# Cross-attention on one core: probabilities times V in bursts of four key tiles instead of two, six slots for exponentials instead of four

## The reference

```python
q = (x @ Wq + bq).reshape(B, N, NUM_HEADS, HEAD_DIM)      # N = 512, 16 heads of 32
k = (y @ Wk + bk).reshape(B, M, NUM_HEADS, HEAD_DIM)      # M = 8192, y has 384 features
v = (y @ Wv + bv).reshape(B, M, NUM_HEADS, HEAD_DIM)
scores = jnp.einsum('bnhd,bmhd->bhnm', q, k) * scale
attn = jax.nn.softmax(scores, axis=-1)
out = jnp.einsum('bhnm,bmhd->bnhd', attn, v).reshape(B, N, IMAGE_DIM)
```

## Time and profile before

| | |
|---|---|
| three runs, median | 3089.53 us (3088.96 to 3091.1) |
| profiled execution, span from first to last instruction | 3087.4 us |
| what lies around the span, against the median | 2.1 us |
| TensorE busy, matmul records | 2999.9 us, 97% of the span |
| VectorE busy | 2224.9 us, 72% |
| GpSimd busy | 1964.1 us, 64% |
| ScalarE busy | 1696.0 us, 55% |

### The profile page before, as it was taken

How to read it: one execution, slowest core, us unless ns; L and a number is a source line. 1 busy time by engine, 2 the same in 40 slices (tenths; PEclk the granted TensorE clock), 3 DMA queues, 4 the chain that set the end, 5 groups by cost and what they waited for, 6 DMA issues and landing times.

```text
span 3087.4 us, 41451 instructions
## 1 busy us (share of the span) xinstructions
PE 2999.9 (97%) x15408; PEld 1839.2 (60%) x15408; DVE 2224.9 (72%) x3416; ACT 1696.0 (55%) x2968; POOL 1964.1 (64%) x678
## 2 busy tenths in 40 slices
PE   7999999999999999999999999999999977899999
PEld 4666666666666666666666666666634333344477
DVE  7777777777777777777777777777746799986653
ACT  1566666666666666666666666666641555330021
POOL 1689898989889898988989898989860000000000
PEclk9999999999999999999999999999999988999999
DMA  5422322233223233232223222232231122224100
GB/s 165 121 53 73 75 75 63 63 77 73 73 53 81 69 97 94 63 85 65 73 52 88 62 73 63 72 84 58 48 136 47 42 69 96 65 72 165 68 14 17
DMA packets 100683, 230.13 MB, mean 75 GB/s; under 512 B 22850, under 2 KB 27970, under 8 KB 99234
## 3 DMA queue, kind: packets, MB, share of 16 engines
q1 hardware_dynamic: 99908, 226.71, 27.1%
q10 hardware_dynamic: 576, 0.79, 0.1%
HBM read 114.46 MB, written 8.06 MB: 40 GB/s over the span
## 4 chain that ended last, share of the span: by engine, by line
PE 91%; DVE 6%; ACT 2%; issue 1%; DMA 0%; SPq 0%; ACTq 0%; DVEq 0%
PE ps L1814 16%; PE ps L1853 15%; PE ps L1840 15%; PE ps L1767 9%; PE ps L1791 9%; PE ps L1798 9%; PE ps L2057 4%; PE ps L2021 4%; PE ps L1865 4%; PE ps L2037 3%; DVE bx L1303 1%; PE ps L1826 1%; PE ps L1822 1%; DVE bx L1249 1%; PE ps L2049 1%
## 5 line engine op out<-in xcount | busy, mean ns | idle before, releaser
L1040 DVE TENSOR_REDUCE pm<-ps 128x1 f32<-128x512 f32 x2048 | 1407.4, 691 | 486.9 <-PE ps L1814 412.3
L1522 ACT ACTIVATE pf<-ps 128x512 f32<-128x512 f32 x2048 | 1216.1, 600 | 722.3 <-PE ps L1840 632.8
L891 POOL TENSOR_TENSOR psum<-psum,pf 128x2048 f32<-128x2048 f32 x254 | 1165.7, 4589 | 107.3 <-ACT pf L1522 94.8
L1814 PE MATMUL ps<-ks,qs 96*128 96x512 f32 x2048 | 844.4, 412 | 4.7 <-DVE pm L1040 2.3
L1840 PE MATMUL ps<-qs,ks 98*128 98x512 f32 x2048 | 812.8, 398 | 2.5 <-ACT pf L1522 2.3
L891 POOL TENSOR_TENSOR psum<-pf 128x2048 f32<-128x2048 f32 x127 | 582.0, 4582 | 42.5 <-ACT pf L1522 41.5
L1814 PEld LDWEIGHTS ps<-ks,qs 96*128 96x128 f32 x2048 | 386.6, 189 | 222.8 <-issue 159.1
L1853 PE MATMUL ps<-pf,V 128*32 128x512 f32 x4096 | 494.2, 600 | 0.0
L1840 PEld LDWEIGHTS ps<-qs,ks 98*128 98x128 f32 x2048 | 390.6, 191 | 49.5 <-ACT pf L1522 11.3
L902 POOL PARTITION_ALL_REDUCE qstat<-qstat x2 | 0.7, 366 | 608.3 <-DVE qstat L1339 608.3
L1791 PE MATMUL ps<-cTh,Wkg 128*128 128x512 f32 x732 | 293.0, 400 | 2.6
(11 more groups left out here) (221 smaller groups left out, 3181.3 us busy)
## 6 DMA issues: line engine op xcount, KB each, us to landing
ks<-KH SPq DMA_DIRECT2D x512, 128.0 KB, 2.4
ks<-KL SPq DMA_DIRECT2D x256, 128.0 KB, 2.4
cT<-in_ctxT SPq DMA_DIRECT2D x32, 768.0 KB, 4.7
Wkg<-wk_rows SPq DMA_DIRECT2D x61, 384.0 KB, 3.0
BC<-bc_rows SPq DMA_DIRECT2D x32, 512.0 KB, 4.8
ring<-in_ffn_w SPq DMA_DIRECT2D x16, 1024.0 KB, 7.8
wA<-in_W_fcT SPq DMA_DIRECT2D x4, 1024.0 KB, 11.3
wB<-in_W_projT SPq DMA_DIRECT2D x4, 1024.0 KB, 7.0
```

The costliest lines, as they stand in the source:

```text
L891: pool.tensor_tensor(acc, before, pf[:, tile % P_SLOTS, :], ALU.add).then_inc(s_sum, 1)
L1040: dve.tensor_reduce(pm[:, n // BLK, n % BLK:n % BLK + 1], src, AX.X, ALU.max).then_inc(s_wfree, 1)
L1522: act.activation(pf[:, tile % P_SLOTS, j * NTOK:(j + 1) * NTOK], ps[:, S_BANK + u % S_BANKS, :], ACT.Exp, scale=SCALE).then_inc(s_exp, 1)
L1814: last = pe.matmul(dst, qs[0:3 * HD, h, t * P:(t + 1) * P], ks[0:3 * HD, keys_of(of, j), i * 512:(i + 1) * 512], start=True, stop=True)
```

## The change

`BURST` goes from 2 to 4 and `P_SLOTS` from 4 to 6. Bursts stand at steps 0 and 16 only, each with four key tiles and the denominators of the run of four tiles before; at steps 8 and 24, where a burst of two tiles with denominators stood, there is none. ScalarE copies the denominators out at step 17 instead of 9 (the condition uses BURST), and D, their transposition, moves from step 16, behind the burst, to step 22. For the last group both keep their places. The last line makes room in on-chip memory for two more slots of `pf`.

```diff
--- before.py
+++ after.py
@@ -71,6 +71,7 @@
 SB_AHEAD = 2
 M_STEP = UPG - 6
 T_LAG = UPG + 15
+D_LAG = 7
@@ -89,8 +90,8 @@
 LOW_AT = {2: (0, 0), 3: (1, 2)}
-P_SLOTS = 4
-BURST = 2
+P_SLOTS = 6
+BURST = 4
 BURSTS = NGT * MT // BURST
 NSUM = 4
 RUNS = NGT * MT // NSUM
@@ -98,7 +99,7 @@
 ADDS = NSUM - 1
 STEPS = (NGT - 1) * UPG + T_LAG + 2
 ATTENDED = UNITS - UPG + T_LAG - UPG + 2
-TURNED = UNITS + BURST * HG + 2
+TURNED = UNITS + 10
@@ -136,8 +137,14 @@
-    if i >= T_LAG and (i - T_LAG) % UPG < 2 and (i - T_LAG) // UPG < NGT:
-        items.append((("T", "D")[(i - T_LAG) % UPG], (i - T_LAG) // UPG))
+    g, r = divmod(i - T_LAG, UPG)
+    if 0 <= g < NGT and r == 0:
+        items.append(("T", g))
+    g, r = divmod(i - T_LAG - D_LAG, UPG)
+    if 0 <= g < NGT - 1 and r == 0:
+        items.append(("D", g))
+    if i == STEPS - 1:
+        items.append(("D", NGT - 1))
     return items
@@ -1565,8 +1572,10 @@
                 if i % UPG == 1 and 1 <= i // UPG <= NGT:
                     take_out(i // UPG - 1)
-                if i % UPG == BURST * HG + 1 and 1 <= i // UPG <= NGT:
+                if i % UPG == BURST * HG + 1 and 1 <= i // UPG < NGT:
                     take_sums(i // UPG - 1)
+                if i == UNITS + 9:
+                    take_sums(NGT - 1)
@@ -2191,7 +2200,7 @@
-    nc = _bacc.Bacc("TRN2", target_bir_lowering=False, num_devices=1)
+    nc = _bacc.Bacc("TRN2", target_bir_lowering=False, num_devices=1, dynamic_dma_scratch_size=256)
```

## The result

| | before | after |
|---|---|---|
| median | 3090.1 us (3089.0 to 3091.1, 4 runs) | 3202.1 us (3201.2 to 3207.9, 4 runs) |
| ratio after / before | | 1.0367, 95% interval 1.0353 to 1.0382 |
| span of the profiled execution | 3087.4 us | 3200.2 us |
| one group, from M to M, mean of 58 | 34.60 us | 36.43 us |
| last M of the loop to the start of the last denominators | 36.7 us | 36.7 us |

The prediction was 3202 us. All of the 113 us between the spans lie in the attention loop: 61 groups that are 1.83 us longer make 112 us, and what comes behind the loop has kept its length.

The account below looks back on a forecast made before the run. TensorE's starts were taken to bound the attention loop. The terms -41 - 10 + 62 + 85 + 16 = +112 us moved the median from 3089.5 to 3202 us, with a range of 3165 to 3240.

Parts of the forecast that it names:

- fewer bursts: Attention loop: bursts fall from 256 to 128, each saving 0.32 us of going in and coming out; 41 us saved.
- V copy at step 0: Denominators follow the four tiles, so the V copy lies beside them and 28 TensorE waits go; 10 us saved.
- hand-over at step 8: Side bank from K to V without a covering burst: V starts 1.0 us late in 62 groups; 62 us lost.
- hand-over at step 24: V starts 1.4 us late behind `KL`, half taken earlier by the A of step 25; 61 groups, 85 us lost.
- D at step 22: Away from a burst, D waits 0.22 us for a reduction and costs 0.26 us more, 62 times; 16 us lost.
- tail: Last two groups and tail: counted at 0 (-3 to +5), having no side work.
- What bounds the kernel: Attention loop: time is the sum of TensorE's starts; nothing else matters until a TensorE item must wait.
- Hidden hand-overs: Rival: the hand-overs at steps 8 and 24 stay hidden and the time falls to 3055 us; 5%.
- only one of them visible: Rival: only one hand-over shows, 3117 us (step 24 hidden) or 3140 (step 8 hidden); 4%.
- GpSimd as the bound: Rival: GpSimd's adds come 1 us late for the burst in each group, 62 us on top, 3264 us; 3%.
- The clock: Rival: TensorE's idling in the attention loop lowers the granted clock to 0.94, about 130 us on top, 3330 us; 3%.

Follow-up runs that it names:

- experiment 8: Experiment 6 with the sign change `nm` of the new maximum done by ScalarE in step 14 instead of VectorE; 3102.3 us.
- experiment 9: Experiment 8 with bursts of two key tiles instead of four; 3127.5 us.
- experiment 1: The changed kernel with bursts of two key tiles again, six slots and D at step 22 kept; 3109.1 us.
- experiment 2: The changed kernel with D moved from step 22 to behind the burst at step 0, ten steps later; 3193.5 us.
- experiment 3: The changed kernel with VectorE computing only the first 128 of 512 columns of `KL`, the rest zero; 3154.3 us.
- experiment 4: The changed kernel with all side work eight steps earlier, K taken out at steps 0 and 16, under the bursts; 3116.2 us.
- experiment 6: Experiment 5 with M moved from step 24 to step 16, ahead of a burst, and A 8 steps further ahead; 3393.4 us.
- experiment 12: Experiment 11 with T moved from step 15 to step 17, behind the burst, D again at step 0; 3088.9 us, ratio 0.9996 to before.
- experiment 5: The changed kernel with experiments 4 and 2 together, VectorE emptying D after `KL`; 3112.5 us.
- experiment 7: Experiment 6 with bursts of two key tiles instead of four; 3335.8 us.
- experiment 11: Experiment 8 with the first three casts of a context half spread over steps and `save_out` behind the keys; 3095.6 us.
- experiment 10: Experiment 6 with the sign change `nm` as a two-input VectorE instruction, -2 x mn + mn; single run, 3395.4 us.

## Why the prediction was right, point by point

| Term | predicted, us | measured |
|---|---|---|
| fewer bursts | -41 | 5.10 us from scores to scores, as worked out; -42 by the ordinary groups of experiments 8 and 9 (0.69 x 61) |
| V copy at step 0 | -10 | before, 28 first K pieces end 0.36 us late (10 us), in the changed kernel none; the 28 waits return in experiment 1 |
| hand-over at step 8 | +62 | 1.01 us late in the timeline, 62 x 1.01 = 63 |
| hand-over at step 24 | +85 | 1.40 us late, 61 x 1.40 = 85, half of it by the A |
| D at step 22 | +16 | 0.20 us in the timeline = 12; 16 in the loop by experiment 2 |
| tail | 0 | 0.4 us |
| sum | +112 | +112.0 (medians), 95% interval 109 to 118 |

**What bounds the kernel.** Right. TensorE's starts set the time, and no other engine became the bound: experiment 3 made one VectorE instruction shorter and the whole of it came off the time only because TensorE waited for that instruction.

**The bursts' saving.** The 0.32 us stand in the trace of after, since the start-to-start distances come out as composed. The medians of experiments 8 and 9 give only 25 us for them, but those kernels differ in three things more, the groups at the change of the batch, the fourth groups and the hand-over of V at steps 8 and 24. Taken from the ordinary groups alone and with the V hand-overs put back it is 0.34 us for a burst. That is worked out from two traces; no run has the bursts' saving by itself.

**The hand-overs.** Right in place, in size and in the split between A and V. Experiment 1 takes both away with the cause, experiment 3 makes them smaller by what `KL` loses, experiment 4 covers them again without touching the bursts.

**D.** Right in kind; the wait is 0.12 us in the timeline against 0.22 predicted. That the sum meets the measured time to within a us is in part luck: D measured 12 to 16 us for 16, and the bursts are known to a few us.

**The rivals.** Hidden hand-overs (3055 us) and only one of them visible (3117 or 3140) fall by the two timelines and by experiment 3, where 0.40 us off `KL` took 0.81 us off each group. GpSimd as the bound (3264) falls: it is busy 1610 of 1900 us where it was 1691, and the sum closes without it. The clock (3330) did not fall: 1.00 with TensorE idle 4.5% of the time, in pieces of at most 0.75 us between records. That the clock can fall in this loop experiment 6 shows, with one pause in each group, up to 3.7 us long.

**Is there a version that wins?** With every hand-over covered, bursts of four reach the time of before (experiment 12) but do not beat it. Experiment 9, the same arrangement with bursts of two, is 37 us over before (3127.5 against 3090.2), though its ordinary group of 34.50 us is no longer than the mean of 34.60 before. About 26 us of it lie in the loop, in every fourth group and in one of 39.0 us, and some 11 in front of the loop. So the arrangement has costs of its own, and they take what the bursts give: in experiment 12 the fourth groups are still 1.1 us over the ordinary ones, and the front is still about 10 us longer.

## What stays open

Why the last group takes longer with D at step 0 and bursts of four, at a lower granted clock (0.76 in experiment 2). From its first scores to the last denominators are 31.6 us before and 33.3 in the changed kernel, but 38.3 and 39.0 in experiments 2 and 5; with bursts of two, D at step 0 costs no such thing (32.0 and 33.4 us in experiments 7 and 9). Open is also whether experiment 12 would be faster than before without its two visible losses, the wait of 1.0 us for GpSimd's low part in 14 groups and the 10 us in front of the loop. That was not tried. The `KL` of the changed kernel was not moved to another engine either, which would be the direct way to a shorter chain.

## What to carry to other kernels

A block of work on the bounding engine can have a second job that no list of waits names: it covers the hand-over of a shared bank between two other units. Before moving it, add up the chain from the end of the bank's last writer to the start of the next one (here, at step 8, 1.6 us through two engines and 0.16 us for TensorE to start again) and compare it with what the bounding engine has to do in between once the block is gone (0.7 us); the difference, worked out for each place with what else stands in front on the same engines and times its occurrences, was the loss to within a few us. And when an instruction moves, look at what its neighbours on the other engines are doing at the new place, GpSimd above all: a 0.17 us instruction of VectorE became 4.2 us long by moving eight steps. And a wait that comes with a long group need not be its cause: in experiment 11 the cast's wait was gone and the fourth groups were no shorter.

## What the runs showed of the hardware that I had not expected

- VectorE's one-input `tensor_scalar` (4.17 us) and two-input `scalar_tensor_tensor` (4.16 us) on 128x16 float32 numbers last until a GpSimd add of 4.6 us ends that started before them (62 of 64 in each of experiments 6 and 10, to 0.04 us); the same work is 0.17 us beside an idle GpSimd and 0.21 us on ScalarE. A reduction of 128x48 numbers took 0.20 us beside the same add.
- The granted clock from 300 to 2200 us stayed 1.00 with pauses between TensorE's records of 0.7 us twice in 36 us (the changed kernel), and with one of 1.2 us in every fourth group (experiment 11). With one pause in each group of 39 us, 3.7 us in most, it averaged 0.94 (experiment 6); right behind such a pause it was 0.50, the lower of the two levels, and matmuls started 0.42 us apart instead of 0.235. The Trainium skill, "TensorE: Matmul & The Clock Gate", section "What's actually happening", says that an idle TensorE falls to 1.2 GHz and comes back with activity. The trace agrees for the long pauses.
- `scalar_tensor_tensor` from PSUM takes 0.74 us for 512 columns and 0.34 us for 128, so by a straight line through the two, an estimate, about 0.2 us of it do not depend on the size.
